# Decoder layer, last stage: the finished tile leaves by ScalarE and GpSimd, and the rounds' products stand in a new order

## The reference, cut to what matters

```python
A_neg = -softplus(A_logit); A_bar = exp(delta * A_neg)
B_bar = (A_bar - 1.0) / (A_neg - SSM_EPS) * B_proj
state = hs * A_full + out * B_full          # write; once after attention, once after the gate
y = layernorm(einsum(state, W_read))        # read 2
g = silu(y_g @ W_gate) * (y_u @ W_up)       # 256 -> 1024
x1 = x1 + state_2                           # residual
out = x1 + layernorm(x1) @ (kern + LoRA_A @ LoRA_B) + bias
```

## Time and profile before

| | us |
|---|---|
| median of three runs | 934.15 |
| lowest, highest | 932.23, 940.61 |
| profiled execution, device time | 931.4 |
| its span on the core | 929.7 |
| a steady round of the last stage | 34.04 |
| rounds 2 to 7 | 677.7 to 882.8 |
| rounds 8 and 9 and the last store | 882.8 to 929.7 |

### The profile page before, as it was taken

One profiled execution on the slowest core, in us unless ns is written; L12 is line 12 of the kernel. 1 busy time (PEld: TensorE's weight loads), 2 busy tenths in 40 slices (PEclk: granted clock), 3 DMA queues, 4 the chain that ended last, 5 costly groups with the idle time before them and its releaser, 6 DMA issues.

```text
span 929.7 us, 15525 instructions
## 1 busy us (share of the span) xinstructions
PE 815.5 (88%) x5786; PEld 425.4 (46%) x5786; DVE 652.8 (70%) x1390; ACT 435.2 (47%) x860; POOL 321.1 (35%) x305
## 2 busy tenths in 40 slices
PE   4899689999999999799986689875689999999987
PEld 2675233333333333366664223224556655656643
DVE  7875457888888886568786567626277778778771
ACT  4465415777677778124244256543333424424410
POOL 2000003777677778210100134443132423423320
PEclk9899899999999999999997577857699999999998
DMA  8664622232322322201225431101001011011011
GB/s 327 239 231 137 185 69 81 77 93 69 109 70 88 90 78 88 80 24 47 76 72 191 160 99 60 48 30 31 1 1 24 24 46 40 6 45 34 1 35 56
DMA packets 75772, 75.81 MB, mean 82 GB/s; under 512 B 37509, under 2 KB 63893, under 8 KB 75062
## 3 DMA queue, kind: packets, MB, share of 16 engines
q1 hardware_dynamic: 75142, 68.77, 23.9%
q10 hardware_dynamic: 560, 6.12, 1.8%
HBM read 53.56 MB, written 21.04 MB: 80 GB/s over the span
## 4 chain that ended last, share of the span: by engine, by line
PE 63%; DVE 15%; ACT 7%; issue 5%; SPq 4%; DMA 3%; POOL 3%; DVEq 0%; ACTq 0%; POOLq 0%; PEldq 0%
PE psum L1693 6%; PE psum L2056 6%; PE psum L1775 5%; PE psum L1826 4%; DVE m_neg L1311 4%; PE psum L2017 4%; PE psum L1883 4%; PE psum L1890 3%; PE psum L1815 3%; PE psum L1836 3%; PE psum L2078 3%; PE psum L1983 3%; SPq L543 2%; PE psum L1961 2%; PE psum L2060 2%
## 5 line engine op out<-in xcount | busy, mean ns | idle before, releaser
L1311 DVE TENSOR_REDUCE m_neg<-psum 128x1 f32<-128x512 f32 x256 | 165.5, 682 | 34.0 <-PE psum L1775 32.0
L933 ACT ACTIVATE region_x<-psum 128x512 f32<-128x512 f32 x256 | 142.7, 597 | 55.5 <-PE psum L1815 54.0
L688 POOL TENSOR_TENSOR region_p<-region_x 128x2048 f32<-128x2048 f32 x32 | 145.2, 4538 | 38.0 <-ACT region_x L933 24.9
L1775 PE MATMUL psum<-ops 96*128 96x512 f16 x256 | 96.6, 386 | 12.6 <-DMA ops<-q_scr 8.0
L1815 PE MATMUL psum<-ops 98*128 98x512 f16 x256 | 95.5, 381 | 0.9 <-ACT region_x L933 0.8
L1693 PE MATMUL psum<-region_x,region_w 128*128 128x512 f16 x320 | 76.7, 397 | 3.0 <-ACT region_w L871 3.0
L1775 PEld LDWEIGHTS psum<-ops 96*128 96x128 f16 x256 | 24.7, 97 | 94.6 <-DVE m_neg L1311 69.1
L1826 PE MATMUL psum<-region_x,v_g 128*32 128x512 f32 x512 | 67.8, 604 | 0.0
L1883 PE MATMUL psum<-sign_o_all,region_a 128*128 128x512 f16 x256 | 60.2, 387 | 3.9 <-DVE region_p L1394 2.8
L2056 PE MATMUL psum<-region_a,c_o 128*128 128x512 f16 x256 | 59.9, 388 | 0.0
L1073 ACT ACTIVATE region_p<-psum 128x512 f32<-128x512 f32 (+2 forms) x96 | 39.1, 463 | 36.7 <-PE psum L1972 36.3
(11 more groups left out here) (253 smaller groups left out, 1615.1 us busy)
## 6 DMA issues: line engine op xcount, KB each, us to landing
ops<-q_scr SPq DMA_DIRECT2D x48, 128.0 KB, 2.5
region_a<-in_x SPq DMA_DIRECT2D x8, 512.0 KB, 9.0
region_a<-in_w_q SPq DMA_DIRECT2D x8, 512.0 KB, 7.4
region_w<-in_w_o SPq DMA_DIRECT2D x8, 512.0 KB, 3.9
region_w<-in_kern SPq DMA_DIRECT2D x16, 256.0 KB, 2.9
kern_scr<-region_w SPq DMA_DIRECT2D x32, 128.0 KB, 1.9
region_p<-in_x SPq DMA_DIRECT2D x8, 512.0 KB, 3.7
region_a<-kern_scr ACTq DMA_DIRECT2D x1, 4096.0 KB
```

The source lines that it names most:

```text
L688: pool.tensor_tensor(pair_sum[:, n], prob_a[:, 2 * n], prob_a[:, 2 * n + 1], ALU.add).then_inc(pair_ready, 1)
L933: act.activation(prob_a[:, kt, j, :], psum[:, (0, 4, 5)[(16 * i + n) % 3], :], ACT.Exp, scale=A_SCALE).then_inc(p_ready, 1)
L1311: dve.tensor_reduce(m_neg[:, i % 3, n:n + 1], psum[:, 1 + (16 * i + n) % 3, :], AX_X, ALU.max, negate=True).then_inc(s_max, 1)
L1775: pe.matmul(psum[:, 1 + (16 * i + n) % 3, :], qa_op[u][0:A_MAX, j, qt * P:(qt + 1) * P], k_op[u][0:A_MAX, :], start=True, stop=True).then_ ...
```

## The change

ScalarE copies the finished tile out of PSUM (`copy_out`, scaled) at the start of a round, and GpSimd adds x1 to it (`residual_out`), after attended of the same round; VectorE's `finish` is gone, and the output's waits count one less. ScalarE copies the turned h_out twice, to fp16 (fT_hi) and to fp32 (into mlpT, which is free between products_2 and the tanh), and VectorE subtracts these two from SBUF in one instruction. The normalisation of tile i-2 moves to the next round, behind write_begin. `to_state` is done a round ahead, behind `dense_lo`. On TensorE the turn of h_out stands before the last two chunks of products_2, the adapters' small sum is in a free quarter of bank 1 instead of bank 5, dense_hi is spread over the round, both dense_lo and the adapters close it, and the gate's products wait for the y2 copies in finer steps.

```diff
+            def residual_out(i):
+                pool.wait_ge(out_copied, i + 2)
+                pool.tensor_tensor(out_t, out_t, x1[:, i, :], ALU.add).then_inc(out_ready, 1)
...
+                if i > 2:
+                    residual_out(i - 3)
+                if i < NT:
                     read_root_2(i)
...
+            residual_out(NT - 2)
...
+            def copy_out(i):
+                act.wait_ge(f_mm, i + 2)
+                act.wait_ge(out_stored, 16 * i + 16)
+                act.activation(out_t.rearrange("p (h n) -> p h n", h=2), psum[:, 4:6, :], ACT.Copy, scale=1.0 / F_GAIN).then_inc(out_copied, 1)
...
             def round_(i, u, first, second, dense, done):
+                if done:
+                    copy_out(i - 3)
                 if first:
                     low_first(i)
                     log_part(0, i)
-                if second:
-                    low_second(i - 1)
                 if dense:
                     act.wait_ge(fT_mm, i - 1)
                     turned(fT_hi, 6, fT_ready)
                 if second:
-                    low_turned(i - 1)
+                    low_second(i - 1)
                 if first:
                     decays(0, i)
+                if dense:
+                    turned(mlpT, 6, fT_ready)
+                if second:
+                    low_turned(i - 1)
...
             def dense_lo(i):
-                dve.wait_ge(fT_ready, 2 * i + 2)
-                for h in range(2):
-                    dve.tensor_tensor(fT_lo[:, 4 * h:4 * h + 4, :], psum[:, 6 + h, :].rearrange("p (c n) -> p c n", c=4),
-                                      fT_hi[:, 4 * h:4 * h + 4, :], ALU.subtract).then_inc(fT_lo_ready, 1)
...
+                dve.wait_ge(fT_ready, 4 * i + 4)
+                dve.tensor_tensor(fT_lo, mlpT, fT_hi, ALU.subtract).then_inc(fT_lo_ready, 1)
...
             def round_(i, u, first, second, dense, done):
-                if done and not first:
-                    finish(i - 3)
-                if dense and not first:
-                    dense_lo(i - 2)
                 if first:
-                    to_mid(i, u, dense, done)
+                    write_begin(0, i)
+                if dense:
+                    to_dense(i - 2)
+                if first:
+                    write_end(0, i, h_in, h_mid[u])
                 if second:
                     write_begin(1, i - 1)
+                if dense:
+                    dense_lo(i - 2)
+                if first and done != LAST:
+                    to_state(i + 1, h_in)
                 if first:
                     read_2(i)
...
                 if second:
-                    to_dense(i - 1)
+                    add_state(i - 1)
...
             write_begin(1, 0)
+            to_state(2, h_in)
             read_2(1)
...
             def gate_up_hi(i, bank, parts=range(2)):
-                pe.wait_ge(y2T_ready, 8 * i + 4)
-
                 for n in parts:
+                    pe.wait_ge(y2T_ready, 8 * i + 2 * n + 2)
...
                 if second:
-                    products_2(range(2, KC))
+                    products_2(range(2, 6))
                 if dense:
                     pe.wait_ge(xf_ready, i - 1)
                     turn(6, h_out, KC, fT_mm)
                 if second:
+                    products_2(range(6, KC))
+                if dense:
+                    adapters_hi(i)
+                if second:
                     turn_low(i - 1)
                 if dense:
...
+                    pe.wait_ge(out_copied, i - 1)
+                    dense_hi(0, range(0, 3))
                 if second:
                     deltas(1, i - 1)
                 if dense:
...
+                    dense_hi(0, range(3, 5))
                 if first:
+                    if dense:
+                        pe.wait_ge(fT_ready, 4 * i - 4)
                     turn_state(i, h_mid[u])
                 if dense:
-                    dense_lo(0, range(3, KC))
+                    dense_hi(0, range(5, KC))
                 if first:
                     read_2(i)
                 if dense:
...
+                    adapters_lo(i)
+                if dense and first:
+                    dense_hi(1, range(0, 5))
                 if first:
                     turn_read(i)
...
+                if dense and first:
+                    dense_hi(1, range(5, KC))
+                    pe.wait_ge(axT_ready, i - 1)
                 if first:
                     gate_up_hi(i, 0)
                     gate_up_lo(i, 0)
                 if dense:
...
+                    dense_lo(0, range(KC))
+                if dense and first:
+                    dense_lo(1, range(KC))
+                    adapters(0)
+                    adapters(1).then_inc(f_mm, 1)
+                if dense and not first:
+                    pe.wait_ge(axT_ready, i - 1)
+                    if second:
                         adapters(0)
+                    else:
+                        adapters(0).then_inc(f_mm, 1)
+                    dense_hi(1, range(KC))
+                    dense_lo(1, range(KC))
                     adapters(1).then_inc(f_mm, 1)
```

More of the change, by code:

```diff
@@ L102 @@
 K_STORED = 32
+LAST = 2
 def build_program(nc, d, out):
@@ L1124, in round_ @@
                     log_part(1, i - 1)
+                if dense:
+                    act.wait_ge(axT_mm, i - 1)
+                    act.activation(axT[0:R2, :], psum[0:R2, 1, P:2 * P], ACT.Copy).then_inc(axT_ready, 1)
                 if first:
@@ L1129, in round_ @@
                 if first:
-                    gate(i, 0)
+                    gate(i, 0, dense)
             act.wait_ge(h2T_mm, 1)
@@ L1625, in to_dense @@
                 dve.tensor_scalar(ves[:], mv[:, 0, 1:2], LN_EPS, None, ALU.add).then_inc(f_step, 1)
+            def to_dense(i):
                 dve.wait_ge(f_rstd, i + 1)
[L1627 to L1634, removed]
+                dve.tensor_scalar(h_out, x1[:, ds(i, 1), :].rearrange("p o n -> p (o n)"), mv[:, 0, 0:1], rstd[:, 0, 0:1],
+                                  ALU.subtract, ALU.mult).then_inc(xf_ready, 1)
             def round_(i, u, first, second, dense, done):
-                if done and not first:
-                    finish(i - 3)
-                if dense and not first:
-                    dense_lo(i - 2)
                 if first:
-                    to_mid(i, u, dense, done)
+                    write_begin(0, i)
[3 more added lines that the diff above has]
+                    write_end(0, i, h_in, h_mid[u])
                 if second:
                     write_begin(1, i - 1)
+                if dense:
+                    dense_lo(i - 2)
+                if first and done != LAST:
+                    to_state(i + 1, h_in)
                 if first:
@@ L1667, in _ @@
             gated(1)
-            to_dense(0)
+            add_state(0)
             run_rounds(dve, round_)
@@ L2100, in adapters, with adapters_hi, adapters_lo @@
                 return pe.matmul(psum[:, 4 + h, :], axT, lora_bt[0:R2 + 1, h * 512:(h + 1) * 512], start=False, stop=True)
+            def adapters_hi(i):
+                pe.wait_ge(fT_ready, 4 * i - 6)
+                pe.wait_ge(lo_loaded, 48 * i - 48)
+                for c in range(KC):
+                    for w in range(2):
+                        pe.matmul(psum[0:R2, 1, P:2 * P], lora_at[:, c, w, :], fT_hi[:, c, :], start=(c == 0 and w == 0), stop=False)
+            def adapters_lo(i):
+                pe.wait_ge(fT_lo_ready, i - 1)
+                for c in range(KC):
+                    mm = pe.matmul(psum[0:R2, 1, P:2 * P], lora_at[:, c, 0, :], fT_lo[:, c, :], start=False, stop=(c == KC - 1))
+                mm.then_inc(axT_mm, 1)
             def round_(i, u, first, second, dense, done):
-                last = not first and not second
                 if first:
```

33 lines of the change are left out of this document (9 added, 24 removed).

## The result

The changed kernel takes 956.9 us (median of four, 956.3 to 957.8), the kernel before 933.2 (median of four) in the runs beside it. The ratio of these runs is put at 1.0235, with a 95% interval of 1.0193 to 1.0277; it is not the plain quotient of the two medians, which is 1.0254. A second comparison gave 953.8 against 934.1, 1.0232 (1.0194 to 1.0271). I had said 935.0, 925 to 944.

A forecast was written before the change was run, and what follows sets the result against it. TensorE bounds the rounds, busy 32.17 of 34.04 us. Opening +0.8, round 2 -0.4, rounds 3 to 6 -1.0, round 7 +0.7, end +2.2 sum to +2.3: forecast 935.0 us, range 925 to 944.

The forecast's parts named there:

- The opening: Before round 1: to_state of tile 2 is put on the path to round 1's first y, costing +0.8 us.
- Rounds 3 to 6: Steady rounds: 33.8 us against 34.04, -0.25 each, -1.0 in all.
- Round 7: Without attended, the residual itself holds up VectorE at write 1; idle 2.55 + 0.48, so +0.7 us.
- The end: Rounds 8 and 9: normalisation waits out the residual, round 9's adapter products begin at +29.2 instead of +27.0; +2.2 us.
- VectorE sees the end of the exp after 0.035 ... L1555 comes first by 0.04: Write 1: VectorE starts before GpSimd, which sees the exp's end after 0.08; the forecast's smallest margin.
- A: End of ScalarE's decay exp in a round, put at E + 5.86 us.
- Any delay of ScalarE helps VectorE: Write 1, argument against rival 1: the exp now comes later, so VectorE has no work left when it ends.
- E: End of the first deltas in a round, 3.85 us into it; the forecast's times count from it.
- rival 1: Write 1: GpSimd is dispatched before VectorE and the residual gets in; 35.8 us a round, +11.2, 942.6 us; chance 0.17.
- the two old waits: TensorE's idle 1.06 us before the adapter products and 0.52 before the gate products; both go, -1.6 a round.
- the new 0.48 at turn_read: TensorE's cover for VectorE's 3.16 us read_2 chain shrinks to 2.72: idle 0.48 a round, 0.65 with the residual.
- to_dense's wait in rounds 8 and 9: VectorE's normalisation waits out GpSimd's residual of 2.2 us each time and ends 0.66 after it.

The follow-up runs named there:

- the filler: Changed kernel plus 14 TensorE matmuls with discarded results right before the turn of the new state, rounds 2 to 7: 948.3 us, ratio 1.0144 to the kernel before.

## Why the prediction was wrong, by its steps

From profile to profile the span grew by 24.9 us. Ahead of round 1's low_first copy, and of everything changed: 6.0, an execution's own. The opening (626.76 to 679.76 before, 632.72 to 686.31 after): +0.6, forecast +0.8. Round 2: -0.2, forecast -0.4. Rounds 3 to 6: +14.0, forecast -1.0. Round 7: +2.3, forecast +0.7. The end, from 882.84 and 905.50: 46.8 to 49.1, +2.3, forecast +2.2.

- **The step that failed** is "VectorE sees the end of the exp after 0.035 ... L1555 comes first by 0.04", in the loop. I had taken the 0.035 from a round written out, and checked a loop round (A to L1555 0.04) only for write 2, where VectorE idles before it. In the loop's write 1 VectorE took 0.12, and GpSimd, at 0.07, was first; in round 7 VectorE took 0.04. That the lag belongs to the loop, where the targets of the waits are computed in registers, follows from the written-out loop, which has the same instructions (0.03). But a wait on a register doesn't cost it by itself: write 2 in the same loop has 0.03, and in the loop with `finish` back, where the exp was already done, the same instruction started 0.54 to 0.56 behind the start of the one in front of it, not 0.66. The lag showed only where the exp ended about 0.54 after that start. What makes it, no row shows.
- **The slack wasn't there.** By its own rows the forecast had VectorE ready at E + 5.89 (0.05 + 2.26 + 0.55 + 1.60 + 1.43), not 5.85, so behind the exp's end at E + 5.86. "Any delay of ScalarE helps VectorE" needs VectorE to be ready first. In the changed kernel's round 6 the exp ended at E + 5.82, and L1570 plus 0.54 gives the same E + 5.82. So rival 1, given 0.17, was what happened.
- **Rival 1 was under-priced**: 35.8 a round, 37.55 measured. The state came at E + 12.1 (E + 12.0 worked out), the idle time was 3.27 (3.1). What I left out was TensorE's clock after such an idle time: 1.45 us a round by the filler. The same is missing in round 7: idle 2.68 (2.55 forecast), and the turn 1.60 for 1.06, the next products 2.64 for 1.46. The forecast's own rows had this price: TensorE's sixteen adapter products take 1.08 in the earlier trace rows, and 1.89 in the earlier trace rows, where TensorE had idled 2.13 us before the turn and 1.85 behind it, and the clock was at 0.50.
- **Right**: the two old waits gone, the new 0.48 at turn_read (0.47; the 0.17 that the residual was to add to it didn't come), the residual's 2.2 (2.33 to 2.36 whole), L1580 waiting for attended when VectorE is first (1.39 to 1.41), the residual between in round 7 (3.01), to_dense's wait in rounds 8 and 9 (2.82), and the gain that all this leaves in a round when the order holds: 33.8 against 33.90. The Trainium skill (SBUF — State Buffer, "Who interferes with whom") puts it that issue order, not the shape of the operation, decides who blocks. The traces agree: the same pair takes 0.96 and 2.50, or 2.50 and 1.73, by 0.05 us.
- **The end** came out right by luck. Counted in us from the start of round 8, that round's last adapter product ended at 23.1 (22.4 forecast, 21.9 before), and in round 9 the first adapter products began at 30.55 (29.2 forecast, 27.0 before). So this part cost 3.55, not 2.2; 0.9 of it is the clock, which behind 4.27 us of idle time made the turn 1.97 us for 1.09. Behind these products, where the forecast had put nothing, 1.3 came back, as the sixteen dense products took 4.24 for 5.54. Before:

```profile
911.66 5.54 PE L2056 MATMUL psum<-region_a,c_o 128*128 128x512 f16 x16
```

and after:

```profile
932.91 1.97 PE L1901 MATMUL psum<-ident,region_p 128*128 128x128 f32 x8 [4.27 <-DVE region_p L1639]
...
937.89 4.24 PE L2067 MATMUL psum<-region_a,c_o 128*128 128x512 f16 x16
```

Before, the granted clock stood at 0.50 for the first 3.3 us of these products (911.66 to 915.00); after, for the first 1.1 (937.89 to 939.00), and in the next microsecond it was 0.92. Why it came back sooner stays open.

## What to carry to other kernels

When work moves to GpSimd, list each VectorE instruction with two SBUF inputs, or the plain fp32 scaling of a tile, that can meet it, and look at what stands directly behind the current GpSimd instruction in its queue: an instruction with a PSUM input between two such is a gap through which it slips. An order that hangs on less than 0.1 us is to be forced by a semaphore, and a lag read in a written-out round, or where the engine idled, need not hold in a hardware loop where the engine has no slack. Before idle time of TensorE is priced, add the clock; and put ready matmuls where the wait is, not where it was.

## What was not expected of the hardware

- In the loop, with its waits on registers, VectorE started 0.12 us behind the exp where that ended about 0.54 us after the start of VectorE's instruction in front; with constants 0.03 to 0.04. Where VectorE had idled 0.84 us, it was 0.03 with registers too.
- After 1.54 or 2.12 us of idle time, TensorE's clock fell in some rounds and not in others with the same instructions: after 1.54 in one of eight loop rounds (34.59 and 35.96), after 2.12 in two of four (35.01 and 36.54). After 3.27 it fell each time. A fall cost 1.4 to 1.5 us.
- The same instructions ahead of the last stage took up to 10 us more or less from one profile to another (first copy at 598.98 to 608.56). The total of the kernel before spread by 13.2 us (928.68 to 941.87) within one set of 19 runs; whether that is the same thing wasn't measured. The cause stays open.
